# Attention scores as 32-row products, half heads across four banks, in two groups of twelve

## What is computed

```python
# x: (4, 1024, 256), context: (4, 77, 256), 16 heads of 16 features
q = (layernorm(x) @ w_q.T + b_q).reshape(B, Nq, H, Dh).transpose(0, 2, 1, 3)
kv = (ctx @ w_kv.T + b_kv).reshape(B, N, H, 2 * Dh).transpose(0, 2, 1, 3)
k, v = (kv[..., :Dh], kv[..., Dh:])
scores = jnp.einsum('bhqd,bhkd->bhqk', q, k) / jnp.sqrt(jnp.float32(Dh))
attn = jax.nn.softmax(scores, axis=-1)
values = jnp.einsum('bhqk,bhkd->bhqd', attn, v)
x = x + values @ w_out.T + b_out
# then: x + experts(layernorm(x)), top 2 of 8, with a layer norm at its end
```

## Time and profile before

| what | us |
|---|---|
| median of 3 runs | 776.0 (774.87 to 776.74) |
| the profiled execution | 775.13 |
| its span, first to last instruction | 773.3 |
| TensorE busy, share of the span | 682.1, 88% |
| VectorE busy, share of the span | 566.8, 73% |
| ScalarE busy, share of the span | 409.8, 53% |
| GpSimd busy, share of the span | 412.0, 53% |

### The profile page before, as it was taken

How to read it: one execution, slowest core, us unless ns; L and a number is a source line. 1 busy time by engine, 2 the same in 40 slices (tenths; PEclk the granted TensorE clock), 3 DMA queues, 4 the chain that set the end, 5 groups by cost and what they waited for, 6 DMA issues and landing times.

```text
span 773.3 us, 15755 instructions
## 1 busy us (share of the span) xinstructions
PE 682.1 (88%) x5640; PEld 651.6 (84%) x5640; DVE 566.8 (73%) x1196; ACT 409.8 (53%) x977; POOL 412.0 (53%) x467
## 2 busy tenths in 40 slices
PE   4899999999999943999999998999999999999500
PEld 3689999999998833999999998999999999999500
DVE  5599898988887787665656679777696676854187
ACT  3255556555555575454444557455474454643185
POOL 6744654564463223536455558657576554632456
PEclk9799999999999955899999999999999999999855
DMA  8400101011010131533353546545455242322484
GB/s 287 166 28 28 43 28 43 33 39 42 29 42 29 43 86 38 173 83 72 68 110 49 100 105 124 114 84 93 100 119 117 44 103 51 58 28 29 63 264 149
DMA packets 55348, 63.85 MB, mean 83 GB/s; under 512 B 9312, under 2 KB 50528, under 8 KB 55136
## 3 DMA queue, kind: packets, MB, share of 16 engines
q0 software_dynamic: 15360, 21.31, 17.3%
q1 hardware_dynamic: 39616, 41.39, 16.7%
q10 hardware_dynamic: 288, 0.00, 0.0%
HBM read 38.96 MB, written 23.72 MB: 81 GB/s over the span
## 4 chain that ended last, share of the span: by engine, by line
PE 83%; DVE 8%; DMA 3%; POOL 2%; issue 2%; ACT 1%; POOLq 0%; SPq 0%; DVEq 0%; ACTq 0%
PE banks L852 18%; PE banks L854 18%; PE banks L853 18%; PE banks L973 8%; PE banks L959 6%; PE banks L947 5%; PE banks L1114 2%; PE banks L1048 2%; DMA sum_rows<-y_sb,slot_ids 1%; PE banks L875 1%; DVE oh_lo L1407 1%; PE banks L999 1%; PE banks L1035 1%; DMA res<-sum_rows 1%; DVE z L1648 1%
## 5 line engine op out<-in xcount | busy, mean ns | idle before, releaser
L581 POOL DMA_INDIRECT sum_rows<-y_sb,slot_ids x80 | 131.9, 1648 | 165.9 <-ACT y_sb L795 149.2
L805 ACT ACTIVATE hraw<-banks,b_now 128x256 f32<-128x256 f32 x320 | 132.2, 476 | 89.7 <-PE banks L854 88.4
L852 PE MATMUL banks<-xT_hi,w_hi 128*128 128x256 f32 x560 | 162.0, 289 | 1.7 <-ACT xT_hi L777 1.7
L854 PE MATMUL banks<-xT_hi,w_lo 128*128 128x256 f32 x560 | 159.1, 284 | 0.0
L853 PE MATMUL banks<-xT_lo,w_hi 128*128 128x256 f32 x560 | 158.8, 284 | 0.0
L852 PE MATMUL banks<-w_hi,h_hi 128*128 128x256 f32 x528 | 148.8, 282 | 2.6 <-issue 1.3
L853 PE MATMUL banks<-w_lo,h_hi 128*128 128x256 f32 x528 | 148.7, 282 | 0.0
L854 PE MATMUL banks<-w_hi,h_lo 128*128 128x256 f32 x528 | 148.5, 281 | 0.0
L1614 DVE TENSOR_TENSOR h_lo<-hraw,h_hi 128x512 fp32r<-128x512 f32 x160 | 114.0, 712 | 5.5
L1612 DVE CAST h_hi<-hraw 128x512 fp32r<-128x512 f32 x160 | 79.6, 498 | 43.8 <-ACT hraw L805 43.4
L852 PEld LDWEIGHTS banks<-xT_hi,w_hi 128*128 128x128 f32 x560 | 106.7, 191 | 2.1 <-issue 2.1
(11 more groups left out here) (191 smaller groups left out, 1426.8 us busy)
## 6 DMA issues: line engine op xcount, KB each, us to landing
w1raw<-in_w1T SPq DMA_DIRECT2D x8, 1024.0 KB, 6.5
w2raw<-in_w SPq DMA_DIRECT2D x8, 1024.0 KB, 6.4
xn_rows<-xn SPq DMA_DIRECT2D x32, 128.0 KB, 1.7
sum_rows<-xn SPq DMA_DIRECT2D x32, 128.0 KB, 1.8
out<-z SPq DMA_DIRECT2D x16, 256.0 KB, 2.2
res<-sum_rows SPq DMA_DIRECT2D x7, 512.0 KB, 8.5
X<-in_x SPq DMA_DIRECT2D x2, 1280.0 KB, 13.8
xg<-xn_rows,slot_ids POOLq DMA_INDIRECT x80, 3.3
```

The lines of the kernel that those rows point to most:

```text
L581: g.indirect_dma_start(sum_rows, bass.IndirectOffsetOnAxis(ap=slot_ids[:, st, 1, q:q + 1], axis=0), y_sb[:, u, q, :], None, bounds_check=N ...
L805: a.activation(hraw[:, j // 2, j % 2, :], banks[:, j // 2, (j % 2) * 256:(j % 2 + 1) * 256], ACT.Silu, bias=b1_now[:, (c // SPE) % 2, j:j ...
L852: t_.matmul(o, a_hi, b_hi, start=first, stop=False)
L854: return t_.matmul(o, a_lo, b_hi, start=False, stop=last)
```

## The change

Each of the six products of a half becomes four over 32 rows and 154 columns (two heads). A group holds twelve: for each of the three terms a four, one product in each row quarter, and each of the four goes into another bank. For that a group mixes the two halves. The first group takes row quarters 0 and 2 of f = 0 and 1 and 3 of f = 1; the second takes the others. The first raises a new semaphore, `half_scored`, for which the second waits, and `scores_done` rises by two after the second. The second group stands right behind the first three probability transposes, ahead of the transposes of values; in step 1 it stands where `scores(1)` stood. `scores()` waits for both subtractions of the tile before (`shifted` at 2t).

```diff
--- before.py
+++ after.py
@@ -31,6 +31,7 @@
     HH = NH // 2
     KC = HH // 2 * NK
     KH = HH * NK
+    KQ = KC // 2
     NJ = 5
     JW = 124
     JS = JW - 1
@@ -230,7 +231,7 @@
             "key_rows_made kT_made w_hi_ready v_hi_made xn1T_hi_made q_hi_made pT_made probs_made valsT_hi_made xn2T_made logits_made router_exp row_made lo_apart lo_made_act "
             "xT_hi_made h_made y_scaled w_hi_made z_made mean16_made act_stats_made "
 
-            "kT_done v_done v_rows_done xn1T_done q_done scores_done pT_done pv_done valsT_done out_done "
+            "half_scored kT_done v_done v_rows_done xn1T_done q_done scores_done pT_done pv_done valsT_done out_done "
...
             "kT_split v_made v_lo_made v_placed k_hi_made wq_split wo_split st1_made mv1_made var1_made xn1_made "
@@ -928,26 +929,40 @@
                     pe.wait_ge(sem("k_hi_made"), 2 * (batch_of(t) + 1))
                     pe.wait_ge(sem("k_lo_made"), 2 * (batch_of(t) + 1))
 
-                def scores(f):
+                def quarters(t, second, qs, b):
+
+                    for n, (qq, kk) in enumerate(((q_hi, KH_hi), (q_hi, KH_lo), (q_lo, KH_hi))):
+                        for h in range(4):
+                            f = (h + second) % 2
+                            rows, at = slice(h * P // 4, (h + 1) * P // 4), (2 * b + f) * KH + h * KQ
+                            m = t_.matmul(banks[:, 2 * f + h // 2, (h % 2) * KQ:(h % 2 + 1) * KQ],
+                                          qq[rows, f, qs], kk[rows, at:at + KQ], start=(n == 0), stop=(n == 2))
+                    if second == 0:
+                        m.then_inc(sem("half_scored"), 1)
+                    else:
+                        m.then_inc(sem("scores_done"), 2)
+
+                def scores():
+
                     if within(t, NT):
                         b = batch_of(t)
                         pe.wait_ge(sem("q_hi_made"), DC * (i + 1))
                         pe.wait_ge(sem("q_lo_made"), DC * (i + 1))
-                        wait(pe, sem("shifted"), 2 * (t - 1) + f + 1)
-                        if f == 0 and values_of_step(t - 1) is not None:
+                        wait(pe, sem("shifted"), 2 * t)
+                        if values_of_step(t - 1) is not None:
                             n, js = values_of_step(t - 1)
                             pe.wait_ge(sem("v_placed"), n * NJ + js[-1] + 1)
-                        if f == 0 and u == 1 and within(i + 1, PAIRS):
+                        if u == 1 and within(i + 1, PAIRS):
                             pe.wait_ge(sem("xn1T_hi_made"), i + 2)
                             pe.wait_ge(sem("xn1T_lo_made"), i + 2)
                         qs = slice(u * P, (u + 1) * P)
-                        for n, (qq, kk) in enumerate(((q_hi, KH_hi), (q_hi, KH_lo), (q_lo, KH_hi))):
-                            for h in range(2):
-                                rows = slice(h * P // 2, (h + 1) * P // 2)
-                                m = t_.matmul(banks[:, 2 * f + h, 0:KC], qq[rows, f, qs],
-                                              kk[rows, ds((2 * b + f) * KH + h * KC, KC)],
-                                              start=(n == 0), stop=(n == 2))
-                        m.then_inc(sem("scores_done"), 1)
+                        quarters(t, 0, qs, b)
+
+                def scores_rest():
+
+                    if within(t, NT):
+                        pe.wait_ge(sem("half_scored"), t + 1)
+                        quarters(t, 1, slice(u * P, (u + 1) * P), batch_of(t))
 
                 def transpose_probs(n):
                     if within(t - 1, NT):
@@ -979,9 +994,9 @@
                 if t == 1:
                     first_values(0)
                     first_values(1)
-                    scores(0)
+                    scores()
                     first_values(2)
-                    scores(1)
+                    scores_rest()
                     first_values(3)
                     first_values(4)
                     pe.wait_ge(sem("v_made"), 1)
@@ -989,8 +1004,10 @@
                         values_product(n)
                     pe.wait_ge(sem("v_placed"), NJ)
                 else:
-                    scores(0)
+                    scores()
                 transpose_probs(0)
+                if t != 1:
+                    scores_rest()
                 if within(t - 2, NT):
 
                     pe.wait_ge(sem("vals_made"), t - 1)
@@ -998,8 +1015,6 @@
                     for c in range(DC):
                         m = t_.transpose(banks[:, TR, c * P:(c + 1) * P], vals[:, c * P:(c + 1) * P], ident[:])
                     m.then_inc(sem("valsT_done"), 1)
-                if t != 1:
-                    scores(1)
                 transpose_probs(1)
                 weigh_values(0)
                 if within(i + 1, PAIRS):
```

## The result

The changed kernel takes 790.8 us (median of four runs, 789.4 to 792.85) against 775.7 us (four runs, 774.87 to 776.74): a ratio of 1.0196, 95% interval 1.017 to 1.0222. Predicted were 791. The profiled execution took 791.13 us, with a span of 789.4 (before 775.13 and 773.3).

What follows compares the result with a forecast made beforehand. TensorE was taken as the bound, with 0.45 us of slack a step before it waits for VectorE; 13.0 for steps 4 to 29, 0.9, 0.2 and 1.0 made 15.1 us, so 791 us, range 783 to 811.

Steps and rivals of the forecast that it cites:

- The size of a group: Twelve narrow score products on TensorE: 0.50 us before the transposes, with loads of fours 0.11 apart, where it was 0.62.
- Rivals 1 and 2: 1: fours load two and two, 812 us, chance 0.17; 2: 32-row products run one by one, near 845, 0.04.
- rivals 3 and 4: 3: VectorE's chain doesn't hold TensorE, 768 us, chance 0.06; 4: it lands between, near 776, 0.04.
- The signal's path: From TensorE's scores_done to VectorE: signal at s+1.54 instead of s+0.69, rowmax at s+1.59, subtraction ended at s+3.21.
- the wake-up: From the end of VectorE's subtraction to TensorE's next product: taken as 0.10 us, range 0.06 to 0.15.
- 0.50 a step, even and odd alike: At L875 or L852 TensorE is 0.50 us later in each of steps 4 to 29: 13.0 us.
- the sum: All delays of the attention stage together: 15.1 us on the profiled 775.1, giving 790.2, as a median 791.
- VectorE's 1.13 for `q_hi`: In odd steps VectorE stood 1.13 us for q_hi, which was to hide its 0.85 of delay.
- Steps 30 and 31: Without L875 or L852, the projection waits for valsT_lo: 0.44 us later each, 0.9 together.
- Step 2: Costs nothing, since VectorE was already late there and TensorE stood 1.22 us for vals.
- step 3: The step before the regular steps 4 to 29: costs some 0.2 us.
- The start: rowmax of tiles 0 and 1 waits for twice as many products: 0.3 to 1.5 us, taken as 1.0.

Runs made afterwards that it cites:

- c2: The changed kernel with rowmax taken over 8 of the 77 scores: 770.2 us, ratio 0.994 to the kernel before.
- the fill: The changed kernel with the three transposes of half 1's first probabilities moved to where TensorE waits, ScalarE's copy moved along: 791.2 us, ratio 1.0196.
- the back-to-back order: The changed kernel with both groups of twelve score products together, ahead of the first probability transposes: 810.0 us, ratio 1.0447.
- f1: The changed kernel with rowmax over 8 keys, steps 0 and 1 in the old form, and half 1's transposes moved into TensorE's wait: 775.6 us, ratio 1.0003.
- the old start: The changed kernel with the old 64-row products and their own signals in steps 0 and 1 only: 786.6 us in a single run.
- c3: The changed kernel with rowmax over 8 of the 77 keys and steps 0 and 1 in the old form: 768.8 us, ratio 0.9918.
- c1: The kernel before with rowmax taken over 8 of the 77 scores: 772.0 us, ratio 0.9958.

## Why the prediction was right

- **The size of a group** (0.50, from loads of fours 0.11 apart): measured 0.50, and two groups start 0.97 apart. Rivals 1 and 2 fell here, rivals 3 and 4 with the waits and the time. Inside the group two terms were off and cancelled: the third four's products start 0.28 after the first's for 0.33 (224.23), and 0.22 pass from there to the transposes for 0.17. The choice of the load's 0.11 as the pace was right; of the stream's 0.07 nothing is to be seen in the starts of the products (224.13, 224.23). By the Trainium skill, "TensorE: Matmul & The Clock Gate" (Part 3), a four would have been about 0.08. That is an estimate. The loads side by side agree with it (four within 0.19 to 0.20 us, where one takes 0.19); the pace doesn't: here each four brings its own weights, and the loads of the fours start 0.11 apart.
- **The signal's path** (s+1.54, `rowmax` s+1.59, subtraction ended s+3.21): measured 1.54, 1.59, 3.22. TensorE resumed at s+3.28 for s+3.31: the wake-up took 0.06 where I took 0.10, and the stand in the records of the products is 0.56, in those of the loads 0.67, for 0.74.
- **0.50 a step, even and odd alike**: measured 0.50 and 0.51. The exact hit has some luck in it: at L876 TensorE is 0.47 late (s+3.28 for s+2.81), and 0.03 more arises behind it, for which the sum had no term. Steps 4 to 29 took 195.50 us before (53.90 to 249.40) and 208.33 after (55.88 to 264.21), 12.8 more for the 13.0 of the sum. Nothing else became late, as worked out: `xn1T_lo` and the small rows stayed ahead of who needs them, and of VectorE's 1.13 for `q_hi` 0.79 was left.
- **Steps 30 and 31** (0.44 each): step 30 is 6.98 for 6.54 (264.21 to 271.19), 0.44, with the projection at s+3.66 for s+3.65. Step 2 cost 0 as said, and step 3 0.29 for 0.2.
- **The start was the term furthest off**: 1.0 in the sum, 1.7 in the profile (step 2 at 39.19 for 37.49), above the upper end of 1.5. The weak step is "the same happens to tile 1 at half the granted clock". It priced the wait of `rowmax` alone. It left out what stands behind it in VectorE's queue in step 1, the `VB` rows, and TensorE's wait for them (1.36), which made it 1.31 late; and it had no term for when the full clock comes back, on which the other 0.4 depend and which differs by 3 us between kernels with the same steps 0 and 1.

The sum was 15.1, and the medians differ by 15.1. The two profiled executions, by which the sum was made, differ by 16.0. So part of the agreement is luck: the terms miss by 0.7 at the start and by 0.3 to 0.4 behind step 30.

The rule of the Trainium skill on PSUM ("TensorEngine Tiling (Array Packing)", Performance Considerations, PSUM Bottleneck), that reading it may become the limit once products are packed, isn't borne out as a matter of throughput: `rowmax` and the subtraction took 0.80 each before and after, and VectorE's busy time fell. As latency it is: these two reads of PSUM are what the chain now goes through in each step (89.65 and 90.48 above), and with one of them 0.58 shorter (c2) the loss was gone.

## What to carry to other kernels

- Before signals are merged or put off, count the slack between the wait that a signal feeds and the engine that comes back for the result. Here it was 0.45 us a step: a delay of 0.57 cost 0.2, one of 0.85 cost 0.5, and the 0.24 us that TensorE saved in the same step were worth something only because they also brought the signal forward.
- A packing that fills more of the array by mixing two halves of the data makes the first half late. Here the consumer was on the way back to the packing engine, and the packing paid only once that consumer was shorter. With the maximum 0.58 us shorter the same change stood at 0.994 of the kernel before instead of 1.0196, where the shorter maximum by itself gave 0.9958. Those two intervals overlap, but the steps are 0.07 to 0.08 us shorter (6.77 and 7.96 for 6.84 and 8.03).
- A tighter order isn't always a faster one: look at the granted clock of every version, in stretches, before its steps are compared.

## What the runs showed of the hardware that was not expected

The granted clock fell to half for 3.4 us at a time in the fill, in the back-to-back order and in the fill with the short maximum (f1), and in no other profile between 46 and 262 us. In the back-to-back order two of the falls lasted 6.8 us. All three have 32-row products in a tighter order than the change's. That alone doesn't explain it: between 38 and 46 us the clock also fell once in the old start and in c3 (3.4 us each) and in c1 (6.8 us), and c1 has the old products in the old order. TensorE's busy time does not tell them apart: the changed kernel with the short maximum was busy all 40.00 us from 80 to 120 at full clock, the fill 13.36 of 13.70 between two falls. What decides it stays open; no run isolates it.

Four loads of 32 rows side by side take 0.19 to 0.20 us, as one does, so narrow products lose nothing to their number here. The next load starts 0.11 us later whether a set of weights covers 32 rows (223.95 and 224.06), 64 (151.62 and 151.73) or 128 (L853 and L854 of c2, 211.74 and 211.85).
